# An audio tower with routed experts on one core: sorted rows of four pages interleaved in DRAM, slots turned into addresses on VectorE

## The reference

```python
gs = jnp.einsum('td,ndm->tnm', flat, wg_s)
us = jnp.einsum('td,ndm->tnm', flat, wu_s)
out = jnp.einsum('tnm,nmd->td', jax.nn.silu(gs) * us, wd_s)
logits = (flat @ router_w).astype(jnp.float32)
probs = jax.nn.softmax(logits, axis=-1)
weights, indices = jax.lax.top_k(probs, TOP_K)
weights = weights / (weights.sum(axis=-1, keepdims=True) + 1e-09)
comb = jnp.sum(jax.nn.one_hot(indices, N_ROUTED) * weights[..., None], axis=1)
g = jnp.einsum('td,edm->tem', flat, wg_r)
u = jnp.einsum('td,edm->tem', flat, wu_r)
h = jax.nn.silu(g) * u * comb[:, :, None]
out = out + jnp.einsum('tem,emd->td', h, wd_r)
```

## Time and profile before

| what | value |
|---|---|
| median of 3 runs | 2204.27 us |
| the three runs | 2220.35, 2204.27, 2199.43 us |
| span of the profiled execution | 2217.8 us |
| attention block, up to about | 1358 us |
| routing block, from the first step to the last scatter | 1358 to 1822 us |
| pages block | 1833 to 2217.8 us |
| PE / DVE / ACT / POOL busy | 1895.1 / 1388.7 / 974.3 / 955.8 us |

### The profile page before, as it was taken

The page is one execution under the profiler, slowest core; times in us unless marked ns, Lnnn a source line. Parts: engine busy times, 40 slices in busy tenths (PEclk is TensorE's granted clock), DMA queues, the critical chain, the costliest instruction groups (busy, mean ns, idle before and its releaser), DMA issues. The chain is left out here.

```text
span 2217.8 us, 48607 instructions
## 1 busy us (share of the span) xinstructions
PE 1895.1 (85%) x14417; PEld 1373.3 (62%) x14418; DVE 1388.7 (63%) x3805; ACT 974.3 (44%) x2062; POOL 955.8 (43%) x1315
## 2 busy tenths in 40 slices
PE   4899999999999999999999983887888868767774
PEld 3676767767776766667666652554545547656663
DVE  3468787877787787877787742655556542434444
ACT  1156565656556565656656551222222214323331
POOL 3034444444344444444444442355555541545555
PEclk7589999999999999999999976799999898989897
DMA  2233333433333333433333325122222216878886
GB/s 70 66 102 133 123 131 122 138 114 125 130 123 131 123 129 122 140 109 123 134 120 130 113 94 128 67 87 86 86 86 86 72 67 201 251 230 255 253 253 197
DMA packets 214514, 291.08 MB, mean 131 GB/s; under 512 B 44854, under 2 KB 176666, under 8 KB 214426
## 3 DMA queue, kind: packets, MB, share of 16 engines
q1 hardware_dynamic: 168634, 183.07, 26.6%
q0 software_dynamic: 18048, 49.31, 7.2%
q10 hardware_dynamic: 27744, 57.68, 6.9%
HBM read 83.25 MB, written 129.69 MB: 96 GB/s over the span
## 5 line engine op out<-in xcount | busy, mean ns | idle before, releaser
L799 DVE TENSOR_REDUCE neg_max<-bank 120x1 f32<-120x376 f32 (+2 forms) x896 | 526.6, 597 | 251.1 <-PE bank L575 249.1
L724 ACT ACTIVATE probs<-bank 128x376 f32<-128x376 f32 (+2 forms) x896 | 452.5, 521 | 305.2 <-PE bank L609 299.7
L575 PE MATMUL bank<-k_rows,q_rows 64*128 64x128 f32 (+2 forms) x1536 | 416.0, 343 | 0.2 <-ACT probs L724 0.2
L609 PE MATMUL bank<-q_rows,k_rows 64*120 64x120 f32 (+2 forms) x1536 | 404.8, 345 | 3.7 <-ACT probs L724 3.4
L918 POOL TENSOR_SCALAR_AFFINE_SELECT probs<-probs 128x512 f32<-128x512 f32 (+1 forms) x384 | 233.2, 626 | 300.9 <-ACT probs L724 300.7
L592 PE MATMUL bank<-causal,own_row 64*120 64x120 bf16 (+4 forms) x1792 | 298.1, 247 | 39.7 <-DVE neg_max L799 23.7
L1721 POOL DMA_INDIRECT x_sorted<-r_normed,route x188 | 183.2, 974 | 204.8 <-DVE route L1572 153.1
L2071 POOL DMA_INDIRECT y_got<-y_sorted,p_route x188 | 181.2, 964 | 195.3 <-issue 194.7
L592 PEld LDWEIGHTS bank<-causal,own_row 64*128 64x128 bf16 (+2 forms) x1792 | 145.8, 116 | 192.1 <-DVE neg_max L799 98.5
L575 PEld LDWEIGHTS bank<-k_rows,q_rows 64*128 64x128 f32 (+1 forms) x1536 | 243.2, 191 | 7.9 <-ACT probs L724 6.1
L609 PEld LDWEIGHTS bank<-q_rows,k_rows 64*128 64x128 f32 (+1 forms) x1536 | 231.5, 184 | 9.3 <-ACT probs L724 6.5
(11 more groups left out here) (204 smaller groups left out, 3803.6 us busy)
## 6 DMA issues: line engine op xcount, KB each, us to landing
x_sorted<-zeros ACTq DMA_DIRECT2D x32, 816.0 KB, 3.9
y_sorted<-zeros ACTq DMA_DIRECT2D x32, 816.0 KB, 4.5
x_rows<-x_sorted SPq DMA_DIRECT2D x51, 512.0 KB
y_sorted<-p_y_rows SPq DMA_DIRECT2D x51, 512.0 KB
q_rows<-q_flat_hi SPq DMA_DIRECT2D x256, 94.0 KB
k_rows<-k_flat_hi SPq DMA_DIRECT2D x256, 94.0 KB
q_rows<-q_flat_lo SPq DMA_DIRECT2D x128, 94.0 KB
k_rows<-k_flat_lo SPq DMA_DIRECT2D x128, 94.0 KB
```

The lines of the kernel that those rows point to most:

```text
L575: last = eng.matmul(ps[0:T[t], m * w:(m + 1) * w], q[rows, slot, t * P:t * P + T[t]], k[rows, slot, 0:w], start=False, stop=(m == len(head ...
L609: last = eng.matmul(ps[0:T[t], m * w:(m + 1) * w], k[64 * c:64 * c + 64, slot, t * P:t * P + T[t]], q[64 * c:64 * c + 64, slot, t * P:S], ...
L724: eng.activation(probs[g % 2][0:T[t], first:first + len(heads), OFF[t]:OFF[t] + w], bank_exp[n % 2][0:T[t], 0:len(heads) * w].rearrange("k ...
L799: eng.tensor_reduce(dst, src, AX.X, ALU.max, negate=True).then_inc(max_taken, 1)
```

## The change

`page_rows` is read in another order, so that row p of pages 4q to 4q+3 lie next to each other in DRAM: partition p's 4 KB are one run. The row of a slot therefore has the address (slot / 512) x 512 + (slot mod 128) x 4 + (slot / 128) mod 4. VectorE works that out with integer operations on a [128, 4, 2] tile before it writes `route`; `SLOT`, the number of counts of `slot_step` in a group, goes from 7 to 11. The address goes to the scatters, to `route_dram` and so to the gathers. Sizes and counts of all DMAs on the program's side, and the order of all engines but VectorE's, are as before.

```diff
-        STATE, SLOT, WEIGHT, TOP = 13, 7, 5, 4
+        STATE, SLOT, WEIGHT, TOP = 13, 11, 5, 4
...
+                def whole_slots(st):
+                    n = tiles(st, 0)
+                    eng.wait_ge(slot_step, st.at(0, SLOT, 6))
+                    eng.tensor_copy(slot_i[:, 0:n, :], slot_f[:, 0:n, :]).then_inc(slot_step, 1)
+
+                def slot_fields(st):
+
+                    n = tiles(st, 0)
+                    eng.wait_ge(slot_step, st.at(0, SLOT, 7))
+                    eng.tensor_scalar(row_in_page[:, 0:n, :], slot_i[:, 0:n, :], P - 1, 2,
+                                      ALU.bitwise_and, ALU.logical_shift_left)
+                    eng.tensor_scalar(page_of_four[:, 0:n, :], slot_i[:, 0:n, :], 7, 3,
+                                      ALU.logical_shift_right, ALU.bitwise_and).then_inc(slot_step, 1)
+                    eng.tensor_scalar(four_start[:, 0:n, :], slot_i[:, 0:n, :], 9, 9,
+                                      ALU.logical_shift_right, ALU.logical_shift_left).then_inc(slot_step, 1)
+
+                def rows_of_four(st):
+                    n = tiles(st, 0)
+                    eng.wait_ge(slot_step, st.at(0, SLOT, 9))
+                    eng.tensor_tensor(row_in_page[:, 0:n, :], row_in_page[:, 0:n, :], page_of_four[:, 0:n, :],
+                                      ALU.bitwise_or).then_inc(slot_step, 1)
+
                 def slots(st):
                     n = tiles(st, 0)
                     if not st.before(0, 2):
                         eng.wait_ge(route_stored[st.b % 2], st.turn(0, 2, 16))
                         eng.wait_ge(scattered[(st.b + 2) % 4], st.turn(-2, 4, 32 * TILES, 32 * TILES))
-                    eng.wait_ge(slot_step, st.at(0, SLOT, 6))
-                    eng.tensor_copy(route[st.b % 2][:, 0:n, 0:2].bitcast(U32), slot_f[:, 0:n, :]).then_inc(slot_step, 1)
+                    eng.wait_ge(slot_step, st.at(0, SLOT, 10))
+                    eng.tensor_tensor(route[st.b % 2][:, 0:n, 0:2].bitcast(I32), four_start[:, 0:n, :],
+                                      row_in_page[:, 0:n, :], ALU.bitwise_or).then_inc(slot_step, 1)
...
                     if group:
-                        slots(st)
+                        whole_slots(st)
                     if nxt:
                         shift_logits(st)
+                    if group:
+                        slot_fields(st)
+                        rows_of_four(st)
+                        slots(st)
                     if group:
                         gated_of(st, 1)
                         hidden_of(st, 1)
...
     def page_rows(rows):
-        return rows.rearrange("(q a p) d -> q p a d", a=4, p=P)
+        return rows.rearrange("(q p a) d -> q p a d", a=4, p=P)
```

More of the change, by code:

```diff
@@ L1191, in routing_phase @@
         slot_f = sb("slot_f", [P, TILES, 2])
+        slot_i, row_in_page, page_of_four = (sb(n, [P, TILES, 2], I32) for n in ("slot_i", "row_in_page", "page_of_four"))
+        four_start = sb("four_start", [P, TILES, 2], I32)
         route = [sb(f"route{p}", [P, TILES, 4]) for p in range(2)]
```

## The result

| | kernel before | kernel after |
|---|---|---|
| median | 2216.03 us (20 runs, 2189.14 to 2230.33) | 2229.3 us (20 runs, 2216.6 to 2247.04) |
| ratio after / before | | 1.0093, 95% interval 1.0066 to 1.0121 |
| span of the profiled execution | 2217.8 us | 2220.7 us |
| first to 23rd group's first scatter | 405.2 us | 416.7 us |
| median period of a group | 18.56 us | 19.37 us |

The change makes the kernel slower by 20.6 us by the ratio (14.6 to 26.8 us, times 2216), by 13.3 us from median to median. The two medians alone give 1.0060, just under the interval of the ratio, so the size of the effect is known to some 7 us only; that it is there is clear of noise. The forecast was +14.5 us, "within 1%".

The account below looks back on a forecast made before the run. Loops of waits, not a full engine, were taken to bound routing (closing on the scatters) and pages. Operations +18.5 and transfers -4 gave +14.5 us on 2204.3, so 2218.8 us, range 2196 to 2236.

Parts of the forecast that it names:

- The bound of the routing block: Routing: a loop of waits closing on the scatters, 18.54 us a group, everything between `slot_sums` and `route` inside it.
- Step 1: Routing: five more VectorE operations a group delay the scatters by 0.84 us, over 22 groups +18.5 us (12 to 33).
- None of 0.84 us is covered: Routing: GpSimd has no other work there but its wait, and PE's marks wait for its last scatter.
- rival B: Routing: new operations are absorbed, PE being late by itself; only the transfers count, -4, 2200 us; chance 0.13.
- Step 2: Pages: with 4 KB packets a store lands 0.2 us sooner, once in two steps: -4 us (nothing to -24).
- The price of packets: Pages: 50 ns for a 1 KB packet, 187 ns for 4 KB by the load; 160 to 190 ns expected.
- the DMA share without gathers: Pages: expected sign that the DMA share falls by some 0.03 to 0.08.
- The 7.3 us a step: Pages: expected sign of about 7.3 us a step in the changed kernel.
- Step 3: Scatters and gathers: 1 KB rows at other addresses, an expert's rows 4 KB apart; taken as costing nothing.
- C: Rival: 4 KB spacing crowds indirect DMAs, 0.17 us on each group's or batch's last; +29 us, 2233 us; chance 0.12.
- The sum: Whole kernel: operations +18.5 and transfers -4 give +14.5 us.
- How the numbers follow: Whole kernel: 1% (22 us) taken as the limit of measurement; within it 0.68, slower 0.25, faster 0.07.

Follow-up runs that it names:

- e13: Kernel before, with ScalarE waiting ahead of the logits copy until the previous group's scatters have landed: 2165.05 us, 1.0443 of before.
- e14: Kernel after, with ScalarE waiting ahead of the logits copy until the previous group's scatters have landed: 2180.65 us, 1.0525 of before.
- e3: Kernel after with four more dependent integer operations ahead of the last slot operation: 2100.07 us, 1.0125 of before.
- e18: Kernel before with the new page layout alone and ScalarE's tanh waiting for gathers hung on the store two steps earlier: 2169.75 us, 1.0447 of before.
- e8: Kernel before with only the page layout changed, slots as they were, on chip B: 2074.2 us, 0.9998 of before.
- e2: Kernel before with only the page layout changed, slots as they were, on chip A: 2074.45 us, 0.9987 of before.
- e15: Kernel after with slots computed ahead of the residual work and ScalarE waiting for the previous group's scatters to land: 2054.05 us, 0.9905 of before.
- e7: Kernel after with ranks, counts and slots computed ahead of the first `gated` and `hidden`: 2051.12 us, 0.9881 of before.
- e16: Kernel after, unchanged, run once more on chip A: 2079.39 us, 1.0026 of before.
- e6: Kernel before, unchanged, run on chip B for its profile: 2077.59 us (one run).
- e10: Kernel before with ScalarE waiting ahead of the logits copy for a `sem_inc` GpSimd makes behind its scatters: 2073.23 us, 0.9997 of before.

## Why the forecast was right, and where it was not

**The bound of the routing block** was read rightly. The forecast left open why the marks are late and said that the loop closes over the scatters. On the first chip PE's router products behind the cast in the earlier trace rows end at 1617.0 us (as modelled) and ScalarE's mark comes at 1623.25. e13 puts a wait for the landing there and gets the same period to 0.08 us and the same distance behind the last scatter to 0.1 us. That TensorE's marks themselves wait for the scatters' landing on the first chip is what this suggests; it is argued from equal distances, not shown.

**Step 1, the operations,** came out by its own arithmetic: 0.83 us in the trace, 0.81 in the median period of the first chip, 0.81 on average in the closed loops, for 0.84. "None of 0.84 us is covered" holds there. 22 x 0.84 = 18.5 us stands against 17.9 in the block of e14 less e13. It holds only while the marks are late: on A, B and C 0.67 of the 0.84 us is covered in the median group and the kernel pays 0.2 to 0.45%. That is near what rival B described, by another way (the marks are on time there), and it is false of the executions that were forecast. That the 40 runs of the result all had the late marks of the three runs read, where its loop holds, is luck of a kind: only rival B, at 0.13, had the operations covered. The fixed distances of the earlier trace rows, which spoke against B, were the right evidence.

The Trainium skill (VectorE: DVE Perf Modes, § The DRAIN you can't avoid) has the next operation wait for the pipe to empty, and adds that one which is not held starts earlier. The trace of after agrees for operations that read the last one's result (0.20 us a start for 0.17 us of work, and e3's 0.79 us for four) while independent ones start 0.07 us apart, so the page's second sentence is the one that fits them.

**Step 2, the transfers.** The price of packets was right (181.5 ns for 4 KB, 187 forecast), the DMA share without gathers fell by 0.06 (0.03 to 0.08 forecast; with gathers it stayed at 0.80). That a store's earlier landing is worth -4 us is neither shown nor refuted: -3.6 us with an interval over zero in e18, -0.02% and -0.13% in e8 and e2. The 7.3 us a step that it named came as 6.89, by an execution whose block was 15.7 us shorter; neither e18 nor the 20 runs bear out that the layout does that. By these three runs the term may as well be 0.

The Trainium skill (DMA: Bandwidth & Descriptors, § Specifications) gives 512 B as the shortest transfer at line rate. The traces do not agree in full: 1 KB in 49.4 ns is 20.7 bytes a ns and 4 KB in 181.5 ns is 22.6, so a 1 KB run gives up 8%. No run shows that the kernel's time gains by it, which is what the page would have said of the time.

**Step 3, the scatters' addresses:** nothing, as forecast. Indirect packets 175.6 ns in routing (177.1 before), 236.4 in the pages (241.0). C, which wanted 0.17 us on the last indirect DMA of each group and batch, is out.

**The sum.** +14.5 was forecast; the closed loops give 15.6 or 17.9 less 3.6, so +12 to +14. On the first chip the medians differ by 13.3 us, 1.2 from the forecast, and the ratio says +20.6 (14.6 to 26.8), with the forecast just below its interval. By the ratio the term that is out of place is the -4 of step 2, which no run shows: with it at nothing the sum is +18.5. Between the two readings nothing decides, since no profile shows the difference (the first chip's pair has 3 us between the spans).

**The step that failed** is the one from the sum to the verdict, in "How the numbers follow": "1% (22 us) is what a measurement of this kernel can tell from no change". It took the spread of three runs, 21 us, for what a comparison can resolve. 20 runs of each kernel resolve 0.3%: the ratio is 1.0066 to 1.0121, so the effect is clear of no change, while the forecast called it a case of none that can be told. The operations in the loop of step 1 were there as written, at 0.81 us a group for 0.84; an effect of +14.5 us on steady fixed distances should have been called a small slowdown. The forecast time is off for the same reason: the median of three runs, 2204.3, stood 12 us below that of 20, so the 2218.8 lies 10.5 us below the 2229.3 measured, though the change was sized well.

## What to carry to other kernels

Before pricing an edit, find out whether its loop is closed: where the start of each engine stands at a fixed distance behind the last DMA of the group before, every operation between counts in full (0.83 us became 0.81 a group), and where the engines overlap, most of it is covered up to the slack, here 0.67 us, and nothing beyond. Do not price the block by the median group alone: here three slower groups and the granted clock in them brought the 3.7 us to 6.6. The same period can be made on purpose with one wait for a DMA's semaphore, which lets a closed loop be measured where the kernel does not show it. And what feeds the slowest DMAs goes first in an engine's order: with the slots ahead of the residual work the kernel gains 1.2%, the added operations cost nothing that can be told, and closing the loop costs only 0.2% (e15 against e7) where it cost 5.0% (e14 against e16).

## What the hardware showed that I had not expected

The same kernel took 2216 us in the 20 runs of the result and 2074 to 2077 on A, B and C. Between the profiles of before and e6, 75 us of it lie in the routing block and 68 in the pages. In the routing block it is marks of TensorE that came behind the indirect DMAs instead of behind the products (19 of 20 waits by "remote", none in e6); in the pages block such waits stand in the first profile too (20 before the tanh, 86 us), but whether they are all of the 68 us was not tested. Why the marks are late is open. With the marks on time, the pages block of before runs its DMA engines at a share of 0.97 (0.94 with the layout alone, over the same 238 us), and still the 4 KB packets give no time that can be told from none. A semaphore increment behind GpSimd's indirect DMAs says nothing of them: in e10 a waiter went on 4.9 us before the last of them had run.
